# Second mixing: the reciprocals of the weight sums move to a PSUM bank, and the second weight's products get two banks instead of three

## Chip, cores, metric

The kernel runs on one core of a Trainium2 chip. The metric is the time of the whole kernel on the device in microseconds (us), a median over runs.

## What is computed

Two layers of graph attention and mixture-of-experts over 3125 nodes with 256 features and 50,000 edges. The change lies in the end of the second graph layer and the norm behind it:

```python
w = ex / denom[dst]
agg = jax.ops.segment_sum(w[:, :, None] * V[src], dst, num_segments=N)
deg = jax.ops.segment_sum(jnp.ones((src.shape[0],), jnp.float32), dst, num_segments=N)
msgs = jnp.where(deg[:, None, None] > 0, agg, V)
out = msgs.reshape(N, H * D) @ Wo + bo
x = out + node_features
mu = jnp.mean(x, axis=-1, keepdims=True)
var = jnp.var(x, axis=-1, keepdims=True)
return (x - mu) / jnp.sqrt(var + 1e-05) * gamma + beta
...
x = x + _L1_gnn_ref(_layernorm(x, axis=-1), ...)
x = x + _L1_ffn_ref(_layernorm(x, axis=-1)[None], ...)[0]
```

The expert layer at the end first needs its router's logits, a product of the normed nodes with a 256 x 32 weight.

## The kernel before

The kernel is a sequence of stages with a block of code for each engine. The engines are kept in order by semaphores alone: every engine works off its own list, written out by hand. A stage begins when all engines have ended the one before. The stage at issue is `mix_second`. It stands behind the edges of the second graph layer, whose sums it finds in `acc1` in SBUF: for each of 25 windows of 128 nodes, 4 sums of softmax weights (one a head) and 256 sums of weighted values. Behind it come `place`, which sorts the nodes by expert, and `feed_second`.

The windows are worked in seven groups, 2, then five times 4, then 3 windows (`GROUPS_OF`, numbered 0 to 6). Group 3 is windows 10 to 13, and so on. What happens to a group:

1. VectorE's `scale` (L2489) multiplies the value sums in `acc1` by `inv`, the reciprocals of the weight sums. `inv` is made once at the start (L2539, L2540), 25 x 4 numbers on each of 128 partitions.
2. GpSimd's `message` masks the nodes' own values `val` with `nz` (L2570, for nodes without edges) and adds them to `acc1` (L2575). For group 0 VectorE does it.
3. TensorE's `multiply_messages` turns each window (`ps_m`, L2703). ScalarE copies it to `mt` (L2639). TensorE multiplies it by the second weight `wo` (L2710) into `ps_y`. A pair of windows shares a bank of `ps_y` (pair 5 is windows 10 and 11), and there are three banks.
4. VectorE's `add_residual` takes each pair out of `ps_y` and adds it to `z` (L2526, "a take" below), which counts up `z_done`, and makes the statistics. ScalarE makes the deviation `std` (L2645), VectorE `rstd` and `shift` (L2515, L2516), ScalarE normalises `z` (L2651), GpSimd weighs it by `gamma` (L2583), VectorE adds the features `x` to give `comb` (L2534), and makes the second norm's statistics.
5. ScalarE normalises again (L2656), TensorE turns the result (`ps_n`), ScalarE copies it to `xs` (L2662), TensorE makes the logits `ps_l` (L2731), ScalarE copies them out (L2696).

The order between groups is fixed. VectorE's round r is: `shift` of the second norm of group r-1, `scale` of group r+3, `add_residual` of r+1, `comb` of r, `shift` of the first norm of r+1, statistics of `comb`. TensorE's round r is: the products of group r+2, then turns and logits of group r-1. ScalarE's round r begins with the deviation of the second norm of r-1 and the copies `mt` of group r+2, alternating with L2656 of r-1, and ends with the logits' copy of r-1. So TensorE opens the products of group r+2 in the round in which VectorE takes group r+1.

A product of pair p may start when the bank it writes is free. With three banks that is when pair p-3 has been taken: `wait(pe, z_done, w // 2 - 2)` in `multiply`, where w is the window and w // 2 the pair.

Of the kernel before, what the change touches and what calls it, by code (L numbers as in the profile page):

```python
# [24 lines left out]
P = 128  # L25
N = 3125
E = 50000
D = 256
DC = D // P
WIN = -(-N // P)  # L30
# [21 lines left out]
H1, F1 = 4, 64  # L52
# [8 lines left out]
class Chain:  # L61
# [23 lines left out]
    def wait(self):  # L85

        self.eng.wait_ge(self.sem, self.value())
# [2322 lines left out]
def mix_second(nc, k, a):  # L2410


    with ExitStack() as ctx:
        def sb(name, shape, dt=F32):
            return ctx.enter_context(nc.sbuf_tensor(name, shape, dt))

        def sem(name):
            return ctx.enter_context(nc.semaphore(name))

        def bank(name):  # L2420
            return ctx.enter_context(nc.psum_tensor(name, [P, BANK], F32))

        NG, RING, AHEAD = len(GROUPS_OF), 4, 3
        wo = sb("wo", [P, DC, D])
# [3 lines left out]
        val = [sb(f"val{b}", [P, WMAX, D]) for b in range(2)]  # L2428
        z = [sb(f"z1_{b}", [P, WMAX, D]) for b in range(2)]
        nz = sb("nz", [P, WIN, H1])  # L2430
        inv = sb("inv1", [P, WIN, H1])
        mt = sb("mt", [P, RING, DC, P])
        xs = sb("xs", [P, RING, DC, P])
        stats = sb("stats1", [P, 2, WMAX, 6])
# [3 lines left out]
        shift = sb("shift1", [P, 2, WIN])  # L2438
        ps_m = [bank(f"ps4_m{i}") for i in range(2)]
        ps_n = [bank(f"ps4_n{i}") for i in range(2)]  # L2440
        ps_y = [bank(f"ps4_y{i}") for i in range(3)]
        ps_l = bank("ps4_l")

        loaded, all_loaded = k.loads_in, k.expect_loads(3)
# [9 lines left out]
        z_done = sem("z1_done")  # L2454
# [20 lines left out]
        def pairs_of(r):  # L2475
            lo, hi = GROUPS_OF[r]
            return range(lo // 2, -(-hi // 2))

        def by_head(x):
            return x.rearrange("p w (h f) -> p w h f", h=H1)  # L2480

        @block.vector
        def _(v):
            c = k.chain_on(v)

            def scale(r):
                lo, hi = GROUPS_OF[r]
                acc = by_head(k.acc1[:, lo:hi, H1:H1 + D])
                c.inc(v.tensor_tensor(acc, acc, inv[:, lo:hi, :].unsqueeze(3).to_broadcast([P, hi - lo, H1, F1]),  # L2489
                                      ALU.mult))  # L2490
                marks["scaled", r] = c.count

            def first_message():
                lo, hi = GROUPS_OF[0]
                vals = by_head(val[0][:, 0:hi, :])
                v.wait_ge(val_in[0], 16)
                c.link(v.tensor_tensor(vals, vals, nz[:, 0:hi, :].unsqueeze(3).to_broadcast([P, hi, H1, F1]), ALU.mult))
                v.tensor_tensor(k.acc1[:, 0:hi, H1:H1 + D], val[0][:, 0:hi, :], k.acc1[:, 0:hi, H1:H1 + D], ALU.add
                                ).then_inc(msg, 1)

            def statistics(which, r, of):
                lo, hi = GROUPS_OF[r]
                for w in range(lo, hi):
                    c.inc(v.bn_stats(stats[:, which, w - lo, :], of(w)))
                c.wait()
                for w in range(lo, hi):
                    ins = v.bn_aggr(mv[:, which, w, :], stats[:, which, w - lo, :])
                    if w < hi - 1:
                        c.inc(ins)
                ins.then_inc(k.ln_var, 1)  # L2510

            def scale_and_shift(which, r):
                lo, hi = GROUPS_OF[r]
                v.wait_ge(k.ln_std, var_no[which, r])
                c.link(v.reciprocal(rstd[:, which, lo:hi], std[:, which, lo:hi]))  # L2515
                v.scalar_tensor_tensor(out=shift[:, which, lo:hi], in0=mv[:, which, lo:hi, 0], scalar=-1.0,  # L2516
                                       in1=rstd[:, which, lo:hi], op0=ALU.mult, op1=ALU.mult).then_inc(shift_ready, 1)

            def add_residual(r):
                base = GROUPS_OF[r][0]  # L2520
                v.wait_ge(xin_in[r % 2], 16 * (r // 2 + 1))
                for pair in pairs_of(r):
                    lo, hi = 2 * pair, min(2 * pair + 2, WIN)
                    v.wait_ge(mm_done, hi)
                    at = z[r % 2][:, lo - base:hi - base, :]
                    v.tensor_tensor(at, ps_y[pair % 3][:, 0:(hi - lo) * D].rearrange("p (w d) -> p w d", d=D), at,  # L2526
                                    ALU.add).then_inc(z_done, 1)
                v.wait_ge(z_done, pairs_of(r)[-1] + 1)
                statistics(0, r, lambda w: z[r % 2][:, w - base, :])

            def add_features(r):
                lo, hi = GROUPS_OF[r]
                v.wait_ge(weighted, hi)
                v.tensor_tensor(k.comb[:, lo:hi, 0:D], z[r % 2][:, 0:hi - lo, :], k.x[:, lo:hi, :], ALU.add  # L2534
                                ).then_inc(mixed, 1)

            c.link(v.tensor_scalar(nz[:, :, :], k.acc1[:, :, 0:H1], 0.0, None, ALU.is_equal))
            marks["nz"] = c.count
            c.link(v.tensor_tensor(inv[:, :, :], nz[:, :, :], k.acc1[:, :, 0:H1], ALU.add))  # L2539
            c.link(v.reciprocal(inv[:, :, :], inv[:, :, :]))  # L2540
            scale(0)
            first_message()
            for r in range(1, AHEAD):
                scale(r)
            add_residual(0)
            scale_and_shift(0, 0)
            for r in range(NG):
                if r:
                    scale_and_shift(1, r - 1)
                if r + AHEAD < NG:  # L2550
                    scale(r + AHEAD)
                if r + 1 < NG:
                    add_residual(r + 1)
                add_features(r)
                if r + 1 < NG:
                    scale_and_shift(0, r + 1)
                v.wait_ge(mixed, r + 1)
                statistics(1, r, lambda w: k.comb[:, w, 0:D])
            scale_and_shift(1, NG - 1)
# [139 lines left out]
        @block.tensor  # L2699
        def _(pe):  # L2700
            def turn(bank, src):
                for c in range(DC):
                    mm = pe.transpose(bank[:, c * P:(c + 1) * P], src[:, c * P:(c + 1) * P], k.ident[:, :])  # L2703
                return mm

            def multiply(w):
                pe.wait_ge(k.tile_copied, before + w + 1)
                wait(pe, z_done, w // 2 - 2)
                for c in range(DC):
                    mm = pe.matmul(ps_y[w // 2 % 3][:, w % 2 * D:(w % 2 + 1) * D], mt[:, w % RING, c, :], wo[:, c, :],  # L2710
                                   start=(c == 0), stop=(c == DC - 1))
                mm.then_inc(mm_done, 1)

            def multiply_messages(r):
                lo, hi = GROUPS_OF[r]
                pe.wait_ge(msg, r + 1)
                for w in range(lo, hi):
                    wait(pe, k.tile_copied, before + w - 1)
                    turn(ps_m[w % 2], k.acc1[:, w, H1:H1 + D]).then_inc(k.tile_turned, 1)
                    if w == 0:  # L2720
                        pe.wait_ge(wo_in, 16)
                    if w > lo:
                        multiply(w - 1)
                multiply(hi - 1)

            def logits(r, w):
                pe.wait_ge(n_used, w + 1)
                wait(pe, l_used, r)
                at = w - GROUPS_OF[r][0]
                for c in range(DC):  # L2730
                    mm = pe.matmul(ps_l[:, at * E1:(at + 1) * E1], xs[:, w % RING, c, :], rwt[:, c, :],  # L2731
                                   start=(c == 0), stop=(c == DC - 1))
                mm.then_inc(l_done, 1)

            def normal(r):
                lo, hi = GROUPS_OF[r]
                for w in range(lo, hi):
                    pe.wait_ge(normed, w + 1)
                    wait(pe, n_used, w - 1)
                    turn(ps_n[w % 2], k.comb[:, w, D:2 * D]).then_inc(n_turned, 1)  # L2740
                    if w > lo:
                        logits(r, w - 1)
                logits(r, hi - 1)

            multiply_messages(0)
            pe.wait_ge(loaded, all_loaded)
            for dc in range(DC):
                mm = pe.transpose(ps_l[:, dc * E1:(dc + 1) * E1], rw[:, dc * P:(dc + 1) * P], k.ident[0:E1, 0:E1])
            mm.then_inc(rwt_t, 1)
            multiply_messages(1)  # L2750
            pe.wait_ge(rwt_ready, 1)
            for r in range(NG + 1):
                if r + 2 < NG:
                    multiply_messages(r + 2)
                if r:
                    normal(r - 1)
# [353 lines left out]
```

## Time and profile before

| | |
|---|---|
| median of 3 runs | 1826.35 us (1823.59 to 1827.79) |
| the profiled execution | 1825.39 us |
| its span in the trace | 1823.7 us |
| mean granted TensorE clock over the span | 0.854 of full |
| `mix_second` in the trace | from about 1596 to 1684 us |
| `feed_second`'s first work on TensorE | 1737.8 us |

All times in the trace count from the start of the span. The span is what the engines' records cover, the profiled execution's own time is 1.7 us more, and the median of the runs is 1 us above that. Matmul records carry a modelled end. "Idle before" in a timeline row is the time in which the engine did nothing ahead of this row, and the name behind the arrow is what it was last waiting for. A row of a timeline merges neighbouring instructions of one line (x4 and so on).

### The profile page before, as it was taken

The numbers are of one execution on the slowest core, as the hardware profiler recorded it, in microseconds if no ns is written. First come the engines' busy times: TensorE is split into PE (matmuls) and PEld (weight loads), VectorE is DVE, ScalarE is ACT, GpSimd is POOL, SyncE is SP. The second block draws the span as 40 slices with busy tenths as digits, with TensorE's granted clock in tenths as the row PEclk, the third lists the DMA queues.
The fourth block names the chain that finished last, engine by engine and source line by source line (L and its number), as shares of the span: only waits on it lengthen the run. The fifth ranks groups of instructions, "written<-read, shape, count | busy, mean of one in ns | idle before, by whom it ended". The sixth has DMA issues, their size and how long they took to land. (4 is left out here: it accounts for less than half of the span.)

```text
span 1823.7 us, 29715 instructions
## 1 busy us (share of the span) xinstructions
PE 1314.4 (72%) x7043; PEld 902.9 (50%) x7043; DVE 1397.3 (77%) x3568; ACT 992.8 (54%) x3802; POOL 1106.1 (61%) x1127
## 2 busy tenths in 40 slices
PE   6346666766666568999886888888888788777086
PEld 5223433434334466777553555555555555455075
DVE  6558888888889862564876899999999999785344
ACT  3345556555555352333252588888888888345043
POOL 3577777777777200574425776767767667474556
PEclk9668877778888758999997699999999999986588
DMA  5566777777776209532247888888888888446392
GB/s 152 154 185 209 216 207 220 214 208 210 221 214 192 82 0 300 198 125 84 93 167 241 267 262 270 273 265 272 271 262 270 268 268 261 137 134 137 146 332 69
DMA packets 176346, 367.26 MB, mean 201 GB/s; under 512 B 28663, under 2 KB 65608, under 8 KB 176052
## 3 DMA queue, kind: packets, MB, share of 16 engines
q0 software_dynamic: 58192, 175.85, 31.7%
q1 hardware_dynamic: 113989, 186.10, 31.0%
q10 hardware_dynamic: 4000, 3.41, 0.6%
q8 instruction: 67, 1.10, 0.2%
q14 instruction: 98, 0.80, 0.2%
HBM read 275.24 MB, written 94.15 MB: 203 GB/s over the span
## 5 line engine op out<-in xcount | busy, mean ns | idle before, releaser
L833 POOL DMA_INDIRECT e_rows<-h_rows,src_col x416 | 399.6, 961 | 138.7 <-issue 119.3
L1111 PE MATMUL e_sum<-e_rows,e_of_dst 128*128 128x264 f32 x832 | 308.6, 499 | 112.8 <-DVE e_rows L932 85.7
L1348 POOL DMA_INDIRECT e_rows<-kv_rows,src_col x320 | 302.7, 946 | 118.8 <-issue 70.3
L1556 ACT ACTIVATE e_rows<-e_rows 128x64 f32<-128x64 f32 x1152 | 281.1, 335 | 0.3
L1111 PEld LDWEIGHTS e_sum<-e_rows,e_of_dst 128*128 128x128 f32 x832 | 165.7, 233 | 177.3 <-DVE e_rows L932 91.4
L1632 PE MATMUL e_query<-q,e_to_dst 128*128 x1248 | 205.0, 295 | 64.3 <-DVE e_rows L1396 45.9
L1486 DVE TENSOR_TENSOR acc<-acc,e_sum 128x260 f32 x393 | 165.5, 421 | 44.7 <-DVE acc L1486 31.6
L1672 PE MATMUL e_sum<-e_rows,e_of_dst 128*128 128x260 f32 x640 | 183.4, 409 | 2.3 <-POOL e_rows L1280 1.7
L1632 PEld LDWEIGHTS e_query<-q,e_to_dst 128*128 128x128 bf16 x1248 | 120.9, 100 | 122.5 <-issue 83.4
L1036 ACT ACTIVATE e_rows<-e_rows 128x32 f32<-128x32 f32 x832 | 181.0, 305 | 0.1
L1348 POOL DMA_INDIRECT x<-kv_rows,src_col x96 | 90.9, 947 | 74.8 <-POOLq L2195 38.1
L2036 POOL TENSOR_SCALAR labels<-labels,typ_no 128x1024 bf16<-128x1024 bf16 x26 | 78.4, 3018 | 80.6 <-DMA labels<-step_typ 80.5
L1672 PEld LDWEIGHTS e_sum<-e_rows,e_of_dst 128*128 128x128 f32 x640 | 108.8, 191 | 24.6 <-DVE acc L1486 10.5
L1389 DVE TENSOR_TENSOR e_rows<-e_rows,e_relation 128x512 f32<-128x512 f32 x160 | 108.9, 681 | 8.5 <-DMA e_rows<-kv_rows,src_col 8.3
L1396 DVE TENSOR_TENSOR e_rows<-e_rows,e_query 128x512 f32<-128x512 f32 x160 | 108.5, 678 | 1.0
L942 DVE TENSOR_TENSOR acc<-acc,e_sum 128x264 f32 x208 | 87.2, 419 | 26.5 <-PE e_sum L1111 22.6
L1625 PEld LDWEIGHTS e_relation<-rel,e_to_typ 64*128 64x128 bf16 x1248 | 50.5, 97 | 95.4 <-issue 54.7
L932 DVE TENSOR_TENSOR e_rows<-e_rows,e_probabilities 128x512 f32<-128x512 f32 x148 | 96.1, 677 | 0.8
L1625 PE MATMUL e_relation<-rel,e_to_typ 64*128 64x64 bf16 x1248 | 75.0, 196 | 28.7 <-issue 8.8
L2053 PE MATMUL ps_h<-xt,w 128*128 128x320 f32 x320 | 91.2, 444 | 5.6 <-ACT hid L2073 3.1
L1556 ACT ACTIVATE x<-x 128x64 f32<-128x64 f32 x380 | 93.2, 334 | 0.1
L2062 PE MATMUL ps_y<-w,hid 128*128 128x256 f32 x400 | 87.6, 380 | 3.2 <-ACT hid L2073 3.2
(433 smaller groups left out, 2790.9 us busy)
## 6 DMA issues: line engine op xcount, KB each, us to landing
step_of<-e_of_dst SPq DMA_DIRECT2D x104, 256.0 KB
e_of_dst<-step_of SPq DMA_DIRECT2D x104, 256.0 KB, 4.2
sorted_rows<-zeros SPq DMA_DIRECT2D x1, 14560.0 KB
comb<-sorted_rows SPq DMA_DIRECT2D x56, 260.0 KB
e_rel<-step_rel SPq DMA_DIRECT2D x26, 512.0 KB, 4.3
step_to<-e_to_dst SPq DMA_DIRECT2D x26, 512.0 KB
e_to_dst<-step_to SPq DMA_DIRECT2D x52, 256.0 KB
e_rows<-h_rows,src_col POOLq DMA_INDIRECT x416
```

What stands on the lines that cost most here:

```text
L833: pool.indirect_dma_start(out=g[t // BATCH % R][:, t % BATCH, :], out_offset=None, in_=k.h_rows[:, :], in_offset=bass.IndirectOffsetOnAxis ...
L932: ins = v.tensor_tensor(vals, vals, pr.unsqueeze(3).to_broadcast([P, GROUP // 2, H, F]), ALU.mult)
L1036: ins = act.activation(x, x, ACT.Copy, scale=row[:, D + h:D + h + 1])
L1111: pe.matmul(psm[t % NB], of_dst[q][:, s % GROUP, :], g[m % R][:, s, :], start=True, stop=True).then_inc(summed, 1)
L1348: pool.indirect_dma_start(out=rows_at(t, 1)[:, 0, :], out_offset=None, in_=k.kv_rows[:, :], in_offset=bass.IndirectOffsetOnAxis(ap=k.src_c ...
L1389: c.inc(v.tensor_tensor(keys, keys, ps_r[q % 2].unsqueeze(2).to_broadcast([P, QP, H, F]), ALU.add))
L1396: v.tensor_tensor(keys, keys, ps_q[q % 2][:, :, :], ALU.mult).then_inc(look_used, 1)
L1486: v.tensor_tensor(acc[:, w[t % 8], :], acc[:, w[t % 8], :], psm[t % NB], ALU.add).then_inc(added, 1)
L1556: ins = act.activation(x, x, ACT.Copy, scale=row[:, plo + h:plo + h + 1])
L1625: mm = pe.matmul(ps_r[q % 2][:, t, :], to_typ[h // 2 % 2][typ, s * P:(s + 1) * P], k.by_typ[typ, j, :], start=(j == 0), stop=(j == 2))
L1632: mm = pe.matmul(ps_q[q % 2][:, t, :], to_dst[h % 2][:, s * P:(s + 1) * P], k.by_dst[:, w[t], j, :], start=(j == 0), stop=(j == 2))
L1672: pe.matmul(psm[t % NB], of_dst[q % GROUPS][:, s % GROUP, :], rows_at(t, 1)[:, 0, plo:R1], start=True, stop=True).then_inc(summed, 1)
```

## The change

`inv` is no longer a tensor in SBUF but lies in a PSUM bank of its own, which only VectorE writes and reads. The core has eight PSUM banks and the stage used them all (two `ps_m`, two `ps_n`, three `ps_y`, one `ps_l`), so `ps_y` gives up its third. With two banks a product of pair p waits until pair p-2 has been taken: `z_done` is waited for at `w // 2 - 1`. Which instruction follows which is the same on each engine in both kernels; the operands of L2539, L2540 and L2489 on VectorE and the bank that L2710 writes and L2526 reads differ, and the count that TensorE waits for.

```diff
--- before.py
+++ after.py
@@ -2428,7 +2428,6 @@
         val = [sb(f"val{b}", [P, WMAX, D]) for b in range(2)]
         z = [sb(f"z1_{b}", [P, WMAX, D]) for b in range(2)]
         nz = sb("nz", [P, WIN, H1])
-        inv = sb("inv1", [P, WIN, H1])
         mt = sb("mt", [P, RING, DC, P])
         xs = sb("xs", [P, RING, DC, P])
         stats = sb("stats1", [P, 2, WMAX, 6])
@@ -2438,7 +2437,8 @@
         shift = sb("shift1", [P, 2, WIN])
         ps_m = [bank(f"ps4_m{i}") for i in range(2)]
         ps_n = [bank(f"ps4_n{i}") for i in range(2)]
-        ps_y = [bank(f"ps4_y{i}") for i in range(3)]
+        ps_y = [bank(f"ps4_y{i}") for i in range(2)]
+        inv = bank("ps4_inv")[:, 0:WIN * H1].rearrange("p (w h) -> p w h", h=H1)
         ps_l = bank("ps4_l")
 
         loaded, all_loaded = k.loads_in, k.expect_loads(3)
@@ -2523,7 +2523,7 @@
                     lo, hi = 2 * pair, min(2 * pair + 2, WIN)
                     v.wait_ge(mm_done, hi)
                     at = z[r % 2][:, lo - base:hi - base, :]
-                    v.tensor_tensor(at, ps_y[pair % 3][:, 0:(hi - lo) * D].rearrange("p (w d) -> p w d", d=D), at,
+                    v.tensor_tensor(at, ps_y[pair % 2][:, 0:(hi - lo) * D].rearrange("p (w d) -> p w d", d=D), at,
                                     ALU.add).then_inc(z_done, 1)
                 v.wait_ge(z_done, pairs_of(r)[-1] + 1)
                 statistics(0, r, lambda w: z[r % 2][:, w - base, :])
@@ -2705,9 +2705,9 @@
 
             def multiply(w):
                 pe.wait_ge(k.tile_copied, before + w + 1)
-                wait(pe, z_done, w // 2 - 2)
+                wait(pe, z_done, w // 2 - 1)
                 for c in range(DC):
-                    mm = pe.matmul(ps_y[w // 2 % 3][:, w % 2 * D:(w % 2 + 1) * D], mt[:, w % RING, c, :], wo[:, c, :],
+                    mm = pe.matmul(ps_y[w // 2 % 2][:, w % 2 * D:(w % 2 + 1) * D], mt[:, w % RING, c, :], wo[:, c, :],
                                    start=(c == 0), stop=(c == DC - 1))
                 mm.then_inc(mm_done, 1)
```

## Rows read from the trace of the kernel before

**Rows 1.** Windows view, all engines (PEclk: granted clock, share of full):

```profile
1596.00:1684.30 88.30, 64.16 (x302) 51.80 (x302) 60.26 (x160) 47.69 (x123) 54.66 (x40) 0.76 0.54 137
1663.00:1684.00 21.00, 15.16 (x66) 12.95 (x66) 8.31 (x30) 12.18 (x31) 9.05 (x4) 0.50 1.02 209
```

**Rows 2.** Table of waits, 1618 to 1664: us in total, times, longest:

```profile
PE ps_y L2710 <- ACT mt L2639: 6.1, 4, 2.2
...
ACT z L2651 <- DVE shift L2516: 3.4, 2, 2.5
```

**Rows 3.** Timeline of TensorE: start us, us, what, idle before and its releaser:

```profile
1606.41 0.66 PE L2703 MATMUL ps_m<-ident,acc 128*128 128x128 f32 x4 [0.53 <-POOL acc L2575]
...
1610.36 1.89 PE L2710 MATMUL ps_y<-wo,mt 128*128 128x256 f32 x8
...
1621.07 1.26 PE L2710 MATMUL ps_y<-wo,mt 128*128 128x256 f32 x4 [1.92 <-ACT mt L2639]
...
1631.38 1.33 PE L2710 MATMUL ps_y<-wo,mt 128*128 128x256 f32 x4 [2.24 <-ACT mt L2639]
...
1642.14 1.83 PE L2710 MATMUL ps_y<-wo,mt 128*128 128x256 f32 x4 [0.99 <-ACT mt L2639]
...
1652.86 2.08 PE L2710 MATMUL ps_y<-wo,mt 128*128 128x256 f32 x4 [0.98 <-ACT mt L2639]
```

**Rows 4.** Timeline of ScalarE:

```profile
1628.71 2.08 ACT L2651 ACTIVATE z<-z,shift,rstd 128x256 f32<-128x256 f32 x4 [0.89 <-DVE shift L2516]
...
1641.53 0.30 ACT L2645 ACTIVATE std<-mv,eps 128x4 f32<-128x4 f32 x1
1641.73 0.35 ACT L2639 COPY mt<-ps_m 128x256 f32<-128x256 f32 x1
```

**Rows 5.** Timeline of VectorE, the takes of groups 3 to 5:

```profile
1632.55 1.28 DVE L2526 TENSOR_TENSOR z<-ps_y,z 128x512 f32<-128x512 f32 x2
...
1643.48 1.28 DVE L2526 TENSOR_TENSOR z<-ps_y,z 128x512 f32<-128x512 f32 x2
...
1653.33 1.28 DVE L2526 TENSOR_TENSOR z<-ps_y,z 128x512 f32<-128x512 f32 x2
```

**Rows 6.** Single lines of code: duration ns min/median/max, first and last start us:

```profile
L2489 DVE TENSOR_TENSOR acc<-acc,inv x7: 691/1211/3391, 1597.2 to 1642.6; 128x1024 f32<-128x1024 f32 x5, 128x512 f32<-128x512 f32 x1, 128x768 f32<-128x768 f32 x1
...
L2526 DVE TENSOR_TENSOR z<-ps_y,z x13: 408/677/692, 1605.7 to 1663.5; 128x512 f32<-128x512 f32 x12, 128x256 f32<-128x256 f32 x1
...
L2498 DVE TENSOR_TENSOR acc<-val,acc x1: 691/691/691, 1599.2 to 1599.2; 128x512 f32<-128x512 f32 x1
...
L2570 POOL TENSOR_TENSOR val<-val,nz x6: 1896/1900/2426, 1601.5 to 1642.6; 128x1024 f32<-128x1024 f32 x5, 128x768 f32<-128x768 f32 x1
...
L2583 POOL TENSOR_TENSOR z<-z,gamma x25: 720/724/1782, 1611.4 to 1670.3; 128x256 f32<-128x256 f32 x25
```

**Rows 7.** Timeline of VectorE, 1609 to 1624:

```profile
1609.17 3.39 DVE L2489 TENSOR_TENSOR acc<-acc,inv 128x1024 f32<-128x1024 f32 x1
1612.49 1.28 DVE L2526 TENSOR_TENSOR z<-ps_y,z 128x512 f32<-128x512 f32 x2
...
1616.37 2.10 DVE L2516 SCALAR_TENSOR_TENSOR shift<-mv,rstd 128x4 f32<-128x4 f32 x1
...
1622.35 1.28 DVE L2526 TENSOR_TENSOR z<-ps_y,z 128x512 f32<-128x512 f32 x2
```

**Rows 8.** Timeline of GpSimd:

```profile
1609.13 2.35 POOL L2575 TENSOR_TENSOR acc<-val,acc 128x1024 f32<-128x1024 f32 x1
1611.44 2.40 POOL L2583 TENSOR_TENSOR z<-z,gamma 128x256 f32<-128x256 f32 x2
...
1615.77 2.67 POOL L2575 TENSOR_TENSOR acc<-val,acc 128x1024 f32<-128x1024 f32 x1
```

**Rows 9.** Windows view of L2710 alone (groups 5 and 2): busy, PEclk:

```profile
1642.10:1648.00 5.90, 5.57 (x16) 0.71 0.00 0
1612.90:1617.20 4.30, 4.05 (x16) 1.00 0.01 2
```

## The prediction

> **What bounds the kernel now.** The change touches one stage of some 88 us, so I read that stage by itself. The windows view gives VectorE 60.3 us and TensorE 64.2 us of work in its 88.3 us, TensorE's at a granted clock of 0.76 in the mean [rows 1]. Neither is full, so the stage is set by a chain that passes between engines, and the table of waits shows which one: from 1618 to 1664 TensorE waits four times for ScalarE's copy `mt` ahead of a product `ps_y`, 6.1 us together, and ScalarE waits only twice for VectorE's `shift` ahead of `z` [rows 2].
>
> The timelines show the cycle behind these waits. TensorE starts the products of a group at 1631.38, the next group's at 1642.14 and the one after at 1652.86 [rows 3]: some 10.7 us for four windows. From the start of the products TensorE works almost without a gap: products, then the turns `ps_n` and the router's products of an older group. ScalarE follows with `xs`, `z`, the logits and then the deviation, issued at 1641.53; right behind it stands, at 1641.73, the copy `mt` that opens the next group [rows 4]. The cycle is TensorE, ScalarE, TensorE. VectorE only hangs on to it: with the deviation it makes `rstd` and `shift`, scales a later group, and only then takes the first pair of the group before, at 1632.55, 1643.48 and 1653.33 [rows 5]. Each of these lies one to two us behind the start of the next group's products.
>
> **The change, part 1: the third bank.** The order of instructions is the same on every engine. What changes is what a product of pair p waits for: VectorE must have taken pair p-2, where it was p-3. Take group 4 (windows 14 to 17, pairs 7 and 8). Pair 7 now waits for pair 5, and pair 5 is the first that `add_residual(3)` takes. Before, it needed pair 4, taken an iteration earlier. So the opening product of each of the groups 3 to 6 now waits for the first of the two takes that the trace shows behind it. Such a take lasts 0.68 us [rows 6], and I allow 0.05 us for the signal, the distance from the end of `mt` at 1642.08 to the product at 1642.14 [rows 3, 4]. The new start, with nothing else moved, is the take's start plus 0.73:
> Group 3: 1622.35 + 0.73 = 1623.08 against 1621.07, late by 2.0 us.
> Group 4: 1632.55 + 0.73 = 1633.28 against 1631.38, late by 1.9 us.
> Group 5: 1643.48 + 0.73 = 1644.21 against 1642.14, late by 2.1 us.
> Group 6: 1653.33 + 0.73 = 1654.06 against 1652.86, late by 1.2 us (no scaling stands ahead of this take).
> The starts are in [rows 3], the takes in [rows 5, 7]. Sum 7.2 us. The lateness adds up from group to group, because what stands behind the waiting product on TensorE is its own group's products and then the older group's turns and router products, for which ScalarE waits, and the deviation that starts the next take is the last thing ScalarE does in that round. Groups 1 and 2 pay nothing: pair 3 needs pair 1, which VectorE took at 1612.49 in the trace of before, with pair 2 right behind, and takes earlier now [rows 7]. The second pair of each group pays nothing either: VectorE takes both pairs in one go, in 1.28 us [rows 7], and the eight matmuls of a pair last 2 us or more [rows 9].
>
> **Part 2: reciprocals in PSUM.** `scale` has both inputs in SBUF now. Seven of them last between 0.69 and 3.39 us, and the median, of the shape that five have, is 1.21 us [rows 6]. The one of 3.39 us starts at 1609.17, 0.04 us behind a GpSimd addition that ends at 1611.48 [rows 7, 8]. The takes of `ps_y`, with one input in PSUM and the rest in SBUF, never pass 0.692 us in 13 [rows 6], and the two at 1612.49 lie beside GpSimd's weighing, which runs to 1613.84 [rows 7, 8]. I read from this that the pair of SBUF inputs is what collides, and that `scale` with `inv` in PSUM will take 1.2 us each time. Length at no collision: the nearest rows are 0.677 for 512 elements with one PSUM input and 0.691 with two in SBUF [rows 6], so nothing is added for reading PSUM; the bounds are -0.1 and +0.5 us for seven scalings and the three small ones at the start (0.07 us each). Two small instructions write PSUM now (the sum and the reciprocal, 100 elements); no row shows that form, and I put them at zero between -0.05 and +0.2 us. The Trainium skill, page "VectorE: DVE Perf Modes", section on the TRN2 errata, gives a fixed cost of 120 cycles for a PSUM source against 58 for SBUF, at 0.96 GHz. By that each scaling would be 0.065 us longer, 0.45 us for seven, of which four are ahead of a take; the rows of 0.677 and 0.691 us speak against it, and the sum leaves it out.
>
> What the relief is worth has to be followed, since 2.18 us of VectorE is not 2.18 us of the end. (a) GpSimd's first masking, at 1601.5, is the longest of six with 2.43 us where the median is 1.90 [rows 6]; without the scalings beside it the first GpSimd message is 0.5 us earlier, and TensorE, which waited 0.53 us for it [rows 3], turns window 2 that much earlier. (b) The scaling at 1609.17 ends near 1610.4, not 1612.56. VectorE then takes pair 1, but pair 2's products end at 1612.25 [rows 3], or 1611.75 with (a), so of 2.18 us some 1.3 us arrive at the statistics, (a) included. (c) `shift` at 1616.37 takes 2.10 us: it has two SBUF inputs, is held behind GpSimd's addition at 1615.77, and ends with it at 1618.44 [rows 7, 8]. It keeps both inputs. So its end is GpSimd's end. That addition can start 0.96 us earlier (weighing two windows took 2.40 us beside the scaling, and is twice 0.72 without [rows 6, 8]), but VectorE's `comb`, 0.7 us with both inputs in SBUF, then falls between two of GpSimd's instructions and holds the second back. I take 0.8 us for the deviation of group 0 and with it the start of group 3's products; the bounds are 0.4 and 1.4.
>
> **Part 3: slack.** After group 3's products ScalarE has copied `xs` and then idles 0.89 us until VectorE's `shift` lets it start `z` at 1628.71 [rows 4]. So TensorE may be 0.9 us late once without effect. The later rounds have no such slack: of ScalarE's two waits for `shift` [rows 2] this is the last.
>
> **The sum.** 7.2 - 0.8 - 0.9 = 5.5 us. Group by group: group 3 late by 1.2, group 4 by 1.2 - 0.9 + 1.9 = 2.2, group 5 by 4.3, group 6 by 5.5, and the stage's end by the same, as nothing behind it has slack (the next stage starts when this one has ended). The profiled execution took 1825.39 us with a span of 1823.7; the median of the runs is 1826.35, 1 us more. Expected: a span near 1829.2 and a median of 1831.8 us.
>
> **The clock.** Group 2's sixteen matmuls of products were busy 4.05 us at a granted clock of 1.00 throughout (2.4 GHz); group 5's sixteen were busy 5.57 us at 0.71 in the mean, so partly at the low level of 1.2 GHz [rows 9]. The fall stands behind a pause of TensorE, and a longer pause moves it, I can't say which way. All at the high level a group takes about 4.0 us, all at the low one twice that. A fall that begins inside the longer pause saves up to 0.8 us a group, a return that comes later costs about 1. I leave it at zero, with -2 and +3 us over the stage as bounds.
>
> **Rivals.**
> 1. Forecast: the wait for the take is serial in each of four rounds; its own range, with the clock's bounds, is 1829.8 to 1834.8 us. Chance 0.66.
> 2. The wait is there, but relief and clock give most of it back: relief at its bound (0.6 us more), the low clock spent in the pauses (2 us), 5.5 - 2.6 = 2.9 us: 1829.2 and below, to 1825. For it: a low stretch that slides into the pause costs nothing. Against: each of three groups has to slide the good way. Chance 0.17.
> 3. Faster, on the other side: the clock no longer falls in the products at all, because the low stretch ends inside the pause. Place: groups 3 to 6 and the tail, which has a clock of 0.50 from 1663 on [rows 1]. Price: 5.6 - 4.0 = 1.6 us for each of four groups, 6.4 us, and an estimated 3 us of the tail, where TensorE works 15.2 us at a clock of 0.50, half of which the high level would spare, less what ScalarE's copies set: 5.5 - 9.4 = -3.9 us, 1822.5 us. It breaks even at 5.5 us, three and a half groups. Against it: the low stretches in the trace came behind pauses and a longer pause would rather bring them than spare them. Chance 0.07.
> 4. Dearer: the clock comes back later in the products (its bound of 3 us), or the changed scaling still collides because `acc` or the output is the cause, so that 3.39 us stay and the 0.8 us of relief are not had: 5.5 + 0.8 = 6.3 to 5.5 + 3 = 8.5 us, 1832.6 to 1834.9 us, and more if both meet. Chance 0.10.
> That the change does nothing to TensorE's wait I leave out: the count it waits for is in the code, and the takes' starts are in the trace.
>
> **How the numbers follow.** What a measurement of this kernel can tell from no change is about 0.2%, 3.7 us, so slower begins at 1830.0 us. Rivals 1 and 4 give 0.76, of which I put 0.06 under that line (of the forecast's low end and the spread of the medians); 0.70 slower. Rival 2 with that part gives 0.22 for no difference, and 0.08 is faster. The range of 8 in 10 is 1828.0 to 1835.5: it takes in the clock's bounds on the forecast and the upper part of rival 2.
>
> **What would show it.** In the trace after, at the opening product of groups 3 to 6, TensorE waits for VectorE's `z` (L2526) and no longer for `mt`, four times, some 2 us more each; from group 4 to group 5 the cycle is 12.8 us, not 10.8, and from 5 to 6 11.9. The scalings of 1024 elements all take 1.2 us; `shift` and `comb` still have single long ones beside GpSimd. The stage's end lies 5 to 6 us later. I would be wrong if the scalings still stretch, if the groups' spacing stays at 10.7 us, or if the granted clock in the products is of another pattern.

## The result

The changed kernel took 1836.47 us in the median of four runs (1832.31 to 1838.56), the kernel before 1826.14. The ratio is 1.0052, with a 95% interval of 1.0038 to 1.0066: some 9.5 us slower. A second set of runs of the same kernel gave 1834.57 us and 1.0044 (1.0029 to 1.0059), 8.0 us. The forecast was slower, 1831.8 us, with a range to 1835.5: the direction holds, the size does not. The first median lies outside the range, the second inside, and both rises are above the 5.5 us that the sum gave.

I call "stage" the stretch from VectorE's first instruction in `mix_second` (L2537) to its first in `place` (L2822). In the traces it takes:

| | before | before, again | after | after, again |
|---|---|---|---|---|
| stage | 88.6 | 90.4 | 96.0 | 96.2 |
| products of group 3 start | 25.3 | 25.7 | 26.0 | 27.1 |
| group 4 | 35.6 | 36.3 | 38.3 | 38.4 |
| group 5 | 46.4 | 48.1 | 51.1 | 51.3 |
| group 6 | 57.1 | 58.8 | 63.5 | 63.6 |
| products, groups 3 to 6 | 5.7, 5.7, 5.7, 4.5 | 4.1, 6.8, 5.7, 4.6 | 6.6, 5.6, 6.0, 5.6 | 5.7, 5.7, 6.1, 5.6 |
| their sum | 21.5 | 21.2 | 23.9 | 23.0 |

All in us, starts counted from the stage's start; "products" is from a group's opening product to the first turn `ps_n` behind them. What lies behind the stage is 139.4 us in the first trace of before and 139.8 in the first after, so the loss that the traces show is in the stage.

### The profile page after: what moved, and what is told of

Its sections match the earlier page's. It is cut to its first block and busy times, and to the rows that moved or that the text cites. A ratio compares the mean times of both kernels' runs of the same rounds, so it can differ in the third digit from the quotient of the medians.

```text
span 1830.6 us, 29717 instructions
## 1 busy us (share of the span) xinstructions
PE 1319.9 (72%) x7043; PEld 907.9 (50%) x7043; DVE 1395.6 (76%) x3568; ACT 992.7 (54%) x3802; POOL 1099.8 (60%) x1127
## 5 line engine op out<-in xcount | busy, mean ns | idle before, releaser
L1672 PE MATMUL e_sum<-e_rows,e_of_dst 128*128 128x260 f32 x640 | 187.2, 415 | 1.4 <-POOL e_rows L1280 0.8
```

The source lines that it names most:

```text
L1672: pe.matmul(psm[t % NB], of_dst[q % GROUPS][:, s % GROUP, :], rows_at(t, 1)[:, 0, plo:R1], start=True, stop=True).then_inc(summed, 1)
```

## The profile after

The table of waits, 1616 to 1664 (us in total, times, longest), answers to [rows 2]:

```profile
PE ps_y L2710 <- DVE z L2526: 12.7, 4, 4.0
...
ACT z L2651 <- DVE shift L2516: 1.8, 1, 1.8
```

TensorE waits four times for a take, 12.7 us, where it waited 6.1 us for `mt`. Ahead of `z` ScalarE waits for `shift` once, where it waited twice; the wait of 0.89 us that was the slack is gone. TensorE's timeline at the four opening products, against [rows 3]:

```profile
1620.73 2.04 PE L2710 MATMUL ps_y<-wo,mt 128*128 128x256 f32 x4 [4.01 <-DVE z L2526]
...
1633.00 2.04 PE L2710 MATMUL ps_y<-wo,mt 128*128 128x256 f32 x4 [3.24 <-DVE z L2526]
...
1645.84 2.05 PE L2710 MATMUL ps_y<-wo,mt 128*128 128x256 f32 x4 [3.14 <-DVE z L2526]
...
1658.22 2.04 PE L2710 MATMUL ps_y<-wo,mt 128*128 128x256 f32 x4 [2.28 <-DVE z L2526]
```

ScalarE at the same two places as [rows 4]. Its `z` follows the copies at once now, and the deviation that starts the take is issued at 1643.07:

```profile
1628.32 2.08 ACT L2651 ACTIVATE z<-z,shift,rstd 128x256 f32<-128x256 f32 x4
...
1643.07 0.30 ACT L2645 ACTIVATE std<-mv,eps 128x4 f32<-128x4 f32 x1
1643.27 0.36 ACT L2639 COPY mt<-ps_m 128x256 f32<-128x256 f32 x1
```

VectorE, against [rows 5, 7]: the scaling that took 3.39 us, `shift` and `comb` beside GpSimd, and three takes.

```profile
1607.53 1.21 DVE L2489 TENSOR_TENSOR acc<-acc,ps_inv 128x1024 f32<-128x1024 f32 x1
...
1614.51 1.52 DVE L2516 SCALAR_TENSOR_TENSOR shift<-mv,rstd 128x4 f32<-128x4 f32 x1
...
1622.95 1.94 DVE L2534 TENSOR_TENSOR comb<-z,x 128x1024 f32<-128x1024 f32 x1
...
1632.18 1.27 DVE L2526 TENSOR_TENSOR z<-ps_y,z 128x512 f32<-128x512 f32 x2
...
1645.01 1.27 DVE L2526 TENSOR_TENSOR z<-ps_y,z 128x512 f32<-128x512 f32 x2
...
1657.39 1.27 DVE L2526 TENSOR_TENSOR z<-ps_y,z 128x512 f32<-128x512 f32 x2
```

From the deviation at 1643.07 the reciprocal, `shift`, a scaling and the take at 1645.01 follow in a row, and TensorE's product starts at 1645.84, 0.83 us behind the take's start. All seven scalings are free of collisions (ns min/median/max, against the first of [rows 6]):

```profile
L2489 DVE TENSOR_TENSOR acc<-acc,ps_inv x7: 686/1208/1215, 1596.2 to 1644.2; 128x1024 f32<-128x1024 f32 x5, 128x512 f32<-128x512 f32 x1, 128x768 f32<-128x768 f32 x1
```

The products alone in the windows view (busy, count, granted clock), groups 3 to 6 and then group 2, against [rows 9]:

```profile
1620.70:1627.40 6.70, 6.24 (x16) 0.59 0.14 33
1633.00:1638.70 5.70, 5.42 (x16) 0.70 0.12 10
1645.80:1651.90 6.10, 5.71 (x16) 0.65 0.18 51
1658.20:1663.90 5.70, 5.46 (x12) 0.52 0.11 34
1611.20:1615.40 4.20, 4.05 (x16) 1.00 0.11 17
```

The same for groups 3, 4 and 6 of the kernel before:

```profile
1620.70:1627.40 6.70, 5.40 (x16) 0.75 0.07 22
1631.30:1637.10 5.80, 5.27 (x16) 0.71 0.34 117
...
1652.80:1657.40 4.60, 4.33 (x12) 0.64 0.00 0
```

Group 4 is alike (0.71 and 0.70). Group 3 has fallen from 0.75 to 0.59 and group 6 from 0.64 to 0.52: nearly all of group 6's products run at 1.2 GHz. Group 3 is not the same in every execution. In the second trace of the changed kernel it stands at 0.70. In the second trace of the kernel before it stands at 1.00, behind the same pause of 1.9 us that preceded the 0.75, and there it is group 4 that falls to 0.57. Group 6 repeats: 0.64 and 0.63 before, 0.52 and 0.50 after.

## The experiments

| kernel | median us | ratio to before (95%) | stage in its trace |
|---|---|---|---|
| after_again | 1834.57 | 1.0044 (1.0029 to 1.0059) | 96.2 |
| two_banks_sbuf | 1836.65 | 1.0058 (1.0041 to 1.0075) | 99.4 |
| takes_first_psum | 1826.65 | 1.0004 (0.9993 to 1.0015) | 92.9 |
| takes_first_3banks | 1828.87 | 1.0009 (0.9994 to 1.0025) | 88.1 |
| filler_psum | 1826.28 | 0.9999 (0.9986 to 1.0011) | 88.0 |
| filler_3banks | 1825.56 | 0.9986 (0.9975 to 0.9998) | 88.6 |
| relief_early | 1827.56 | 0.9997 (0.9984 to 1.0009) | 90.1 |
| takes_first_z3 | 1824.52 | 0.9986 (0.9974 to 0.9998) | 89.8 |
| scale_behind_takes | 1834.35 | 1.0040 (1.0025 to 1.0056) | 97.3 |
| z3_filler | 1824.48 | 0.9987 (0.9975 to 1.0000) | 86.9 |
| z3_filler_tail | 1821.91 | 0.9975 (0.9965 to 0.9986) | 85.4 |
| before_again | 1825.83 | 1.0001 (0.9992 to 1.0011) | 90.4 |

Each ratio is to the kernel before in the same set of runs. The kernels stand in three sets of four, in the order of the table; the kernel before had medians of 1826.96, 1827.14 and 1826.50 us in them. A stage in one trace is one execution, and the kernel before alone gives 88.6 and 90.4. So differences under 2 us rest on the ratios.

**The same kernels once more.** 

> The changed kernel itself, for a second trace and a tighter time. In the first trace the second mixing takes 96.0 us from VectorE's first instruction to the next stage's first, against 88.6 before: +7.5 us, where the time of the whole kernel is up 10 us in the median. Theory (the stage's clock): where the low clock falls in the four groups' products differs from run to run, so this trace shows the same four waits for VectorE's take, but a stage that is 1 us or more off 96.0, with the difference in the length of the products. Rival (elsewhere): the stage is 96.0 within 0.5 us again, and the other 3 us are in the spread of the stages before it. Time: ratio 1.004 to 1.006.

> The kernel before once more: a second trace of its stage. Theory: 88.6 us within 1.5 us, with the low clock somewhere in each of the groups 3 to 5; ratio 1.000.

The stage of the changed kernel came out the same, within 0.2 us, against the first theory's expectation; the clock's part repeats too (23.0 and 23.9 us of products against 21.2 and 21.5). The second trace of the kernel before missed what was expected of it: its stage is 1.8 us longer than the first, and the low clock is in groups 4 to 6 but not in group 3. Against it the changed kernel's stage is only 5.6 and 5.8 us longer. The rest of the difference in time is not located: the spans of the changed kernel, 1830.6 and 1832.9, lie 6.5 to 9.2 us above those of before, 1823.7 and 1824.1, and the stage explains 5.6 to 7.7.

**One part of the change alone: two banks.** The reciprocals stay in SBUF.

```diff
-        ps_y = [bank(f"ps4_y{i}") for i in range(3)]
+        ps_y = [bank(f"ps4_y{i}") for i in range(2)]
...
-                wait(pe, z_done, w // 2 - 2)
+                wait(pe, z_done, w // 2 - 1)
```

> Two banks for ps_y, the reciprocals left in SBUF: the loss without the relief. Theory (wait for the take, relief worth 1.3 us ahead of group 3's products and little later): the scaling of 3.39 us is back, the stage is 1 to 2.5 us longer than with the change, 97 to 98.5 us, ratio to before 1.005 to 1.007. Rival (the longer stage comes from reading or writing the reciprocals in PSUM): stage near 88.6 us, ratio 1.000.

The loss is all in this part: 1.0058, and 99.4 us (97 to 98.5 expected). But the expectation was wrong on the scaling. Two scalings beside GpSimd take 4.06 us together, where they took 2.35 in the first trace of before, and the one that took 3.39 us there takes 1.21:

```profile
1600.77 4.06 DVE L2489 TENSOR_TENSOR acc<-acc,inv 128x1024 f32<-128x1024 f32 x2
...
1611.26 1.21 DVE L2489 TENSOR_TENSOR acc<-acc,inv 128x1024 f32<-128x1024 f32 x1
```

Which scaling meets GpSimd depends on when `val` has landed. GpSimd's first masking waits for that load. It starts 1.7 us behind the pair of scalings in the first trace of before, well into the second of them, and 0.3 us behind their start here. The second trace of before has the 4.06 us too. With the reciprocals in PSUM the stage is 3.2 us shorter, but 1.7 us of that are shorter products (24.7 us here, 23.0 there). In the time it is 2.1 us between the medians of one set, and the intervals overlap, so it can't be told from nothing.

**The other part alone: relief.** The early scalings read the reciprocals from a `ps_n` bank that is not used yet; three `ps_y` banks.

```diff
+        inv_p = ps_n[1][:, 0:WIN * H1].rearrange("p (w h) -> p w h", h=H1)
...
+                of = inv_p if r <= AHEAD else inv
```

> The relief alone: three banks for ps_y as before, and the reciprocals in the second ps_n bank, which is free until the first turn of normed rows, for the scalings of groups 0 to 3; those of groups 4 to 6 read a copy in SBUF (one copy of 100 numbers more on VectorE). Theory (relief is worth 1.3 us ahead of group 3's products and the rest is loss by the bank): stage 87 to 88 us, ratio 0.999 to 1.000. Rival (the relief is worth more, or reading PSUM costs something that the loss hides): over 1.5 us off that in either direction.

0.9997: no difference can be told, and the trace's 90.1 us lie inside the spread of before, above the 87 to 88 expected. The two early scalings take 2.34 us together, against 4.06 in the second trace of before, but the interval allows from 2.9 us of gain to 1.6 us of loss. A relief of the 0.8 us that the sum had would not be seen in it.

**The place of the take.** On VectorE the takes go ahead of the wait for the deviation; their statistics stay where they were, in a function of their own (`first_statistics`). The control does the same with three banks.

```diff
+                if r and r + 1 < NG:
+                    add_residual(r + 1)
                 if r:
                     scale_and_shift(1, r - 1)
                 if r + AHEAD < NG:
                     scale(r + AHEAD)
-                if r + 1 < NG:
+                if r == 0:
                     add_residual(r + 1)
+                if r + 1 < NG:
+                    first_statistics(r + 1)
```

> The changed kernel, but from round 1 on VectorE takes the pairs of group r+1 ahead of the wait for the second norm's deviation and of the scaling, when it is idle anyway; the statistics stay where they were. Theory (the product waits only because the take stands behind deviation, shift and scaling on VectorE): the waits for z at groups 5 and 6 go, those of groups 3 and 4 shrink to what the load of xin still holds back (0 to 2 us each), stage 88 to 91 us, ratio 0.999 to 1.002. Rival (the bank or the take itself is slow): four waits of 3 us stay, ratio 1.005.

> The same move of the takes in the kernel before, with three banks and the reciprocals in SBUF: the control. With three banks no product waits for a take, so by the theory the move alone is worth nothing (stage 88.6 within 0.7 us, ratio 0.999 to 1.001). Rival (VectorE's order is itself a bound): shorter by over 1.5 us.

With two banks no loss can be told any more (1.0004), and with three the move is worth nothing (1.0009, the interval holds 1). So what two banks cost in the time comes from the place of the take in VectorE's list. The trace alone would not have shown it. The profiled execution was the slowest of twelve (1832.64 us), its stage took 92.9 us, and TensorE still waits 8.3 us for three takes (3.7, 2.7 and 2.0 us for groups 3 to 5). The waits shrank less than expected, since the early takes now wait for a load:

```profile
1624.73 1.29 DVE L2526 TENSOR_TENSOR z<-ps_y,z 128x512 f32<-128x512 f32 x2 [2.80 <-DMA z<-xin_rows]
...
1635.63 1.29 DVE L2526 TENSOR_TENSOR z<-ps_y,z 128x512 f32<-128x512 f32 x2 [1.88 <-DMA z<-xin_rows]
...
1647.32 1.29 DVE L2526 TENSOR_TENSOR z<-ps_y,z 128x512 f32<-128x512 f32 x2 [2.77 <-DMA z<-xin_rows]
```

With a third `z` buffer, and the loads a round earlier:

> The changed kernel with the takes ahead of the deviation's wait, and a third z buffer so that the loads of xin come a round earlier. With two z buffers the early takes waited for those loads (2.8, 1.9 and 2.8 us). Theory: the takes of rounds 1 to 5 come at once, no product of groups 3 to 6 waits for a take, the two banks cost nothing, and the relief is left: stage 86.5 to 88.5 us, ratio 0.999. Rival (two banks cost in another way than by the place of the take): stage over 90 us.

0.9986, and in the table of waits TensorE waits for no take ahead of a product:

```profile
PE ps_y L2718 <- ACT mt L2647: 5.8, 6, 1.9
```

The stage, at 89.8 us, is above what I expected (86.5 to 88.5). The same third buffer with three banks was not run, so a small cost of the second bank could hide behind what the earlier loads give.

**Only the scaling moved behind the takes.**

```diff
-                if r + AHEAD < NG:
-                    scale(r + AHEAD)
                 if r + 1 < NG:
                     add_residual(r + 1)
+                if r + AHEAD < NG:
+                    scale(r + AHEAD)
```

> The changed kernel with only scale moved from ahead of add_residual (takes and statistics) to behind it, in every round. Theory (the product waits for reciprocal, shift, scaling and take in a row): the waits of groups 3, 4 and 5 are shorter by the scaling, 1.1, 1.1 and 0.9 us; but the scaling then delays comb and its statistics; stage 96.1 - 3 = 93 us, ratio to before 1.002 to 1.003. Rival (only the take itself matters): waits unchanged, ratio 1.005.

The waits of groups 3 to 5 are 2.88, 2.38 and 2.28 us, 0.9 to 1.1 us shorter each, as the theory has it, but group 6's stays at 2.27 and the time hardly moved (1.0040, where 1.002 to 1.003 was expected). In round 0 the scaling now stands behind the statistics and comes late, GpSimd's message behind it, and `shift` is held behind that message:

```profile
1617.65 1.19 DVE L2489 TENSOR_TENSOR acc<-acc,ps_inv 128x1024 f32<-128x1024 f32 x1
...
1619.56 2.10 DVE L2516 SCALAR_TENSOR_TENSOR shift<-mv,rstd 128x4 f32<-128x4 f32 x1
```

Group 3's products start at 29.6, 3.6 and 2.4 us later than in the two traces of the changed kernel. Only a part of that is the moved scaling's. Group 2's products already start at 20.2, against 16.5 and 18.7, and they do not need that scaling; in this trace the products of two windows of group 1 ran at a granted clock of 0.52 and took 3.59 us where 1.9 to 2.0 is usual. From group 2 to group 3 it is 9.4 us, against 9.5 and 8.4. So this trace confirms the shorter waits. Why the whole kernel gains nothing that can be told stays open.

**The clock.** Unread products in TensorE's pause, so that it does not stop while it waits.

```diff
+                        if w == lo + 1:
+                            for _ in range(FILL[r]):
+                                pe.matmul(ps_n[0][:, 0:D], k.ident[:, :], wo[:, 0, :], start=True, stop=True)
                         multiply(w - 1)
```

> The changed kernel with extra products that nobody reads (the identity by half of wo, into the first ps_n bank) in TensorE's pause ahead of the opening product of groups 3 to 6: 7, 6, 6 and 4 of them, 3.3 to 1.9 us at the high level. The wait for the take stays. Theory (part of the loss is the low clock, which falls because TensorE pauses for 2.3 to 4 us): the granted clock stays at 1.00 in the products, each group's products take 4.0 to 4.5 us, not 5.6 to 6.6; stage 96.1 - 6 = 90 us, ratio to before about 1.001. Rival (the clock is not set by this pause): products as long as before, and the extra ones only push them, stage 96 us or more, ratio 1.005.

> The kernel before (three banks, reciprocals in SBUF) with 3, 4, 2 and 2 such extra products in its pauses of 1 to 2.2 us. Theory: the clock stays up here too, up to 1.6 us a group, 88.6 - 5 = 84 us for the stage, ratio 0.997. Rival (the thin router products of the older group pull the clock down, not the pause): the low stretches stay, stage 88.6 us, ratio 1.000.

Each such product leaves two matmul records, so seven fillers are the x14 below. In the changed kernel the granted clock stays at 1.00 in the real products of all four groups (columns as above):

```profile
1622.00:1626.10 4.10, 3.93 (x16) 1.00 0.00 0
1631.60:1635.70 4.10, 3.93 (x16) 1.00 0.01 4
1643.70:1647.70 4.00, 3.80 (x16) 1.00 0.00 0
1654.00:1656.90 2.90, 2.83 (x12) 1.00 0.00 0
```

Three of the four opening products still wait for the take, as the timeline with the first filler shows:

```profile
1617.87 3.19 PE L2726 MATMUL ps_n<-wo,ident 128*128 128x256 f32 x14
1622.06 1.10 PE L2711 MATMUL ps_y<-wo,mt 128*128 128x256 f32 x4 [1.00 <-DVE z L2527]
...
1631.66 1.10 PE L2711 MATMUL ps_y<-wo,mt 128*128 128x256 f32 x4 [0.65 <-DVE z L2527]
...
1654.02 1.10 PE L2711 MATMUL ps_y<-wo,mt 128*128 128x256 f32 x4 [0.56 <-DVE z L2527]
```

and yet the stage is 88.0 us (90 expected), and the whole kernel as fast as before (0.9999). Ahead of group 5 the fillers themselves last past the take. The products' stretches add up to 14.7 us, where they were 23.0 and 23.9, and the stage is 8.1 us shorter. So the low level in the products cost the changed kernel's stage some 8 us.

In the kernel before the fillers gave 0.9986 and no shorter stage in the trace (88.6 us, where 84 was expected). The products take 16.0 us there, 5.5 less, but now a turn waits for GpSimd:

```profile
1632.46 0.66 PE L2704 MATMUL ps_m<-ident,acc 128*128 128x128 f32 x4 [1.86 <-POOL acc L2576]
...
1635.15 1.13 PE L2711 MATMUL ps_y<-wo,mt 128*128 128x256 f32 x4 [0.30 <-ACT mt L2640]
```

So the two causes do not add up like terms of a sum. Each remedy alone, the early takes or the fillers, takes away the whole loss. With fillers in both, two banks and three differ by 0.6 us in the stage and 0.7 us in the medians of one set: the waits for the take are still there and cost next to nothing. The reason is not shown by a run of its own; the rows above show only that with three banks the shorter products run into another wait, for GpSimd.

**Both together.** Early takes, third `z` buffer, fillers of 3, 3, 2 and 2 products; and then 5, 3 and 3 more ahead of the last three groups' turns.

> Early takes, third z buffer, two ps_y banks, reciprocals in PSUM, and 3, 3, 2, 2 unread products in the pauses of TensorE ahead of groups 3 to 6. Theory (two separate gains, the wait and the clock): no wait for a take and all products at a granted clock of 1.00, stage 83 to 85.5 us, ratio 0.996 to 0.998, better than both kernels. Rival (with the pauses down to 1 to 2 us the clock falls for another reason): stage 88 us or more.

> The same with 5, 3 and 3 unread products more, ahead of the last three groups' turns of normed rows, where the clock stands at 0.50 in every trace so far. Theory: the clock stays at 1.00 there too and the stage is 2 to 3 us shorter than with the four groups alone. Rival: the tail is paced by ScalarE and VectorE, under 1 us.

z3_filler: all engines from 1620 to 1660 and from 1660 to 1683; granted clock third from the end. Then z3_filler_tail:

```profile
1620.00:1660.00 40.00, 35.02 (x190) 28.83 (x188) 35.87 (x99) 27.04 (x72) 24.57 (x24) 0.91 0.32 91
1660.00:1683.00 23.00, 15.16 (x66) 12.95 (x66) 8.26 (x32) 13.19 (x35) 11.12 (x9) 0.52 1.00 203
```

```profile
1620.00:1660.00 40.00, 34.65 (x195) 28.39 (x196) 36.76 (x102) 27.66 (x73) 24.70 (x25) 0.96 0.30 93
1660.00:1683.00 23.00, 19.67 (x88) 16.23 (x87) 9.22 (x32) 13.50 (x35) 12.15 (x12) 0.70 1.03 214
```

z3_filler fell short of what was expected, 83 to 85.5 us and 0.996 to 0.998. Its products stand at 1.00 in groups 3 and 4 but at 0.83 and 0.79 in groups 5 and 6, so fillers of 3, 3, 2 and 2 are not enough there. It does not differ from takes_first_z3 in the time (0.9987 and 0.9986), though its stage is 2.9 us shorter in the traces. With the tail's fillers the clock in the tail rises from 0.52 to 0.70, not to the 1.00 expected, and the stage falls to 85.4 us, by 1.5 us where 2 to 3 was expected. With 0.9975 (1821.91 us) this has the lowest median of all, 4.6 us under the 1826.50 us of the kernel before in the same set of runs. It is faster than both kernels; its interval overlaps those of z3_filler and takes_first_z3.

## Why the prediction was wrong

*The third bank.* Right: four waits for the take, each added to the last. Between the products of groups 4 and 5 the forecast was 12.8 us, and 12.84 and 12.85 were measured. Between 5 and 6, 11.9 was forecast and 12.4 measured, of which the longer products of group 5 are 0.4. The first traces of both kernels can be compared round by round, with the difference in the products' lengths taken out. Group 3 is then late by 0.7 us, groups 4, 5 and 6 add 1.0, 2.1 and 1.3, and nothing is added behind them: 5.1 us, where the forecast had 1.2, 1.0, 2.1, 1.2 and nothing. The four pairs of traces, taken the same way, give from 2.9 to 6.2 us, so the agreement of the total leans on one pair. One small size was off: the product starts 0.82 to 0.83 us behind the take's start, not 0.73.

*The relief.* The scalings went to 1.215 us at most, as forecast, and PSUM reads cost nothing that shows: 1.208 us in the median against 1.211 [rows 6]. The Trainium skill, page "VectorE: DVE Perf Modes", section on the TRN2 errata, would have made each scaling an estimated 0.065 us longer for its PSUM source. That is not borne out for these instructions, which have one input in PSUM and one in SBUF. The collision that the sum priced, 3.39 us in one scaling, was the case of one execution: the other traces with the reciprocals in SBUF have it in the early pair. The 0.8 us before group 3 came out as 1.3 us in the first trace: its products start 0.7 us late, where 1.2 was forecast. In the second they are 1.8 us late, with the start of the stage itself drawn out by a load.

*The slack.* The 0.9 us were there in the second trace (groups 3 to 4 in 11.28 us, 1.0 more than the 10.31 of before, as forecast) and eaten by the longer products of group 3 in the first (12.27 us).

*The clock.* This is the step that failed, the term "I leave it at zero". The products of groups 3 to 6 took 23.9 and 23.0 us instead of 21.5, so 2.4 and 1.5 us for the term (2.7 and 1.8 against the second trace of before). Groups 5 and 6 are longer in every pair of traces, group 5 by 0.4 us and group 6 by 1.0 to 1.1. 5.5 + 2.4 = 7.9 and 5.5 + 1.5 = 7.0 us come within 0.7 us of the 7.5 and 7.7 that the stage grew over the first trace of before. Over the second it grew by 5.6 and 5.8 only, so the term's size is known no better than between 1.5 and 2.7 us. The bound of +3 us held it, but I set the forecast near the middle of a range whose two sides were not equally likely: the trace had falls only behind pauses, and rival 3 said itself that a longer pause would rather bring them. The fillers show that the low level hangs on the pause: with the pause filled, it is gone from the products. They show too that a sum was the wrong form for it, since the waits cost next to nothing once the clock is high.

*The range.* The stage's +7.5 us on 1826.35 would be 1833.9 us, inside it. The runs' median was 2.6 us above that, the second set's 0.7. That part is not explained by any trace here and stays open; single runs spread over more (1831.5 to 1838.6 over both sets).

*The rivals.* Rival 4 came true by its clock half, though not its collision half. Rivals 2 and 3 needed a clock that falls less than before; in the two traces of the changed kernel it fell more, and it stayed up in all four groups only where fillers held it.

## What to carry to other kernels

When a buffer is taken away, look at where the instruction that frees it stands in its engine's list: a bank fewer cost 8 to 9.5 us because the take stood behind a wait, a norm and a scaling, and nothing that could be told once it stood ahead of them. Relieving an engine that waits for the others is worth what reaches the cycle, here too little to be told from nothing for some 2 us of relief. And where TensorE paces a stage and its clock is partly low, price each longer pause at the low clock as well. Do not add such prices up unchecked: here either remedy alone brought back the whole loss, and both together little more. And trace a kernel twice before you price one stretched instruction.

## What the runs showed of the hardware

A VectorE instruction with two SBUF inputs contends with a GpSimd instruction that reads SBUF (the Trainium skill states this, page "SBUF — State Buffer", section "Who interferes with whom"). The traces agree, and the delay is long: the scaling of 3.39 us, issued 0.04 us behind GpSimd's addition, ended 1.1 us after that addition's end at 1611.48, which is about its whole length without a collision (1.21 us). What I had not expected is that which instruction is hit changes from one execution to the next with the landing of a load: 3.39 us in one trace for a scaling that takes 1.21 or 1.22 in the four others with its reciprocals in SBUF, while these have 4.06 us for the early pair that takes 2.35 in the first. With one input in PSUM no scaling was hit (1.216 us at most in the eight traces of kernels with `inv` in its own bank).

The same pause does not always bring the same clock. Behind a pause of 1.9 us the granted clock in group 3's products was 0.75 in one execution of the kernel before and 1.00 in the other. Seven unread products (fourteen records) in a pause of 4 us kept the granted clock of the sixteen records behind it at 1.00, where it was 0.59 and 0.70, and cut them to 3.93 us of busy time from 6.24 and 5.28.
